# Cross-attention block: the probabilities-times-values products on 64x32 tiles of the PE array instead of 128x64 tiles with zeros in the weights

## What is computed

```
q  = layer_norm(x, ln1) @ wq + bq          # 16 heads x 32
k  = context @ wk + bk ; v = context @ wv + bv
s  = q_h . k_h / sqrt(32), masked where key > query position
p  = softmax(s)
o  = concat_h(p_h @ v_h)                   # the products that are changed
x1 = x + o @ wo + bo
y  = x1 + gelu(layer_norm(x1, ln2) @ w1 + b1) @ w2 + b2
```

## Time and profile before

| | |
|---|---|
| median of 3 runs | 1918.54 us |
| profiled execution, its own time | 1918.34 us |
| its span, first to last instruction | 1916.6 us |
| PE busy | 1820.8 us (95% of the span) |
| DVE / ACT / POOL busy | 1247.4 / 631.8 / 447.1 us |
| mean granted TensorE clock | 0.976 |

### The profile page before, as it was taken

The page is one execution under the profiler, slowest core; times in us unless marked ns, Lnnn a source line. Parts: engine busy times, 40 slices in busy tenths (PEclk is TensorE's granted clock), DMA queues, the critical chain, the costliest instruction groups (busy, mean ns, idle before and its releaser), DMA issues.

```text
span 1916.6 us, 26803 instructions
## 1 busy us (share of the span) xinstructions
PE 1820.8 (95%) x10206; PEld 852.2 (44%) x10214; DVE 1247.4 (65%) x1908; ACT 631.8 (33%) x786; POOL 447.1 (23%) x380
## 2 busy tenths in 40 slices
PE   3737999999999999999999999999999999999999
PEld 2313444444444444444444444444444444444444
DVE  5757967657576766757676665667666566766632
ACT  3434624223242422324242332424233242424211
POOL 1431314122131313213141212213141121413200
PEclk7868999999999999999999999999999999999999
DMA  7051231313323140322314042232404123230300
GB/s 280 9 124 34 44 89 23 77 35 62 72 45 88 23 88 24 69 64 44 89 26 86 23 83 51 45 88 37 96 2 88 45 50 84 45 88 8 60 23 22
DMA packets 287511, 116.48 MB, mean 61 GB/s; under 512 B 262376, under 2 KB 263952, under 8 KB 287376
## 3 DMA queue, kind: packets, MB, share of 16 engines
q1 hardware_dynamic: 287376, 114.61, 26.9%
HBM read 31.22 MB, written 16.78 MB: 25 GB/s over the span
## 4 chain that ended last, share of the span: by engine, by line
PE 89%; DVE 5%; issue 2%; DMA 2%; ACT 1%; POOL 1%; SPq 1%; DVEq 0%; POOLq 0%; ACTq 0%
PE ff_ps L1065 34%; PE ff_ps L1270 33%; PE at_ps L1065 16%; PE at_ps L1209 2%; PE at_ps L1189 2%; DMA arena<-qT 1%; DVE w_all L784 1%; DVE ssum L1006 0%; DMA arena<-in_L_xattn_wv 0%; DVE maxima L793 0%; DVE arena L784 0%; DVE xhat L773 0%; DVE stats L751 0%; DVE arena L990 0%; DVE smax L988 0%
## 5 line engine op out<-in xcount | busy, mean ns | idle before, releaser
L1065 PE MATMUL ff_ps<-arena,w_all 128*128 128x512 f16 x3072 | 701.9, 381 | 11.0 <-ACT arena L709 4.9
L1270 PE MATMUL ff_ps<-w_all,arena 128*128 128x512 f16 x3072 | 697.9, 379 | 1.7 <-DVE arena L784 1.7
L1065 PEld LDWEIGHTS ff_ps<-arena,w_all 128*128 128x128 f16 x3072 | 299.2, 98 | 378.9 <-issue 19.7
L1270 PEld LDWEIGHTS ff_ps<-w_all,arena 128*128 128x128 f16 x3072 | 294.4, 98 | 356.0 <-issue 3.0
L709 ACT ACTIVATE arena<-ff_ps,b1p,scales 128x512 f32<-128x512 f32 x256 | 198.7, 776 | 659.4 <-PE ff_ps L1065 659.1
L1038 DVE TENSOR_SCALAR arena<-arena,scales 128x512 f16<-128x512 f32 x256 | 140.9, 550 | 239.7 <-ACT arena L709 239.7
L784 DVE SCALAR_TENSOR_TENSOR arena<-arena,scales 128x512 f16<-128x512 f32 x256 | 240.1, 938 | 9.1
L477 POOL TENSOR_TENSOR rstd<-ve,minus_half 128x1 f32<-128x1 f32 x128 | 85.8, 671 | 561.7 <-DVE ve L756 554.3
L644 ACT ACTIVATE norm_hl<-xhat 128x512 f16<-128x512 f32 x120 | 73.9, 628 | 294.9 <-DVE xhat L773 294.9
L531 POOL TENSOR_TENSOR x_sb<-x_sb,bo_row 128x512 f32<-128x512 f32 x64 | 90.9, 1450 | 343.9 <-PE at_ps L1189 343.9
L536 POOL TENSOR_TENSOR arena<-arena,rsum 128x1024 f32<-128x1024 f32 x64 | 124.8, 1971 | 180.6 <-DVE rsum L1009 180.6
(11 more groups left out here) (133 smaller groups left out, 1416.3 us busy)
## 6 DMA issues: line engine op xcount, KB each, us to landing
x_sb<-in_x SPq DMA_DIRECT2D x64, 256.0 KB, 2.7
out_x<-arena SPq DMA_DIRECT2D x64, 256.0 KB, 2.3
w_all<-in_L_xattn_w SPq DMA_DIRECT2D x6, 1024.0 KB, 14.8
arena<-in_L_xattn_w SPq DMA_DIRECT2D x2, 1024.0 KB, 14.0
v_sb<-v_sb SPq DMA_DIRECT2D x6, 192.0 KB, 3.1
arena<-in_ctx SPq DMA_DIRECT2D x1, 1024.0 KB, 5.4
arena<-in_L_xattn_wk SPq DMA_DIRECT2D x1, 1024.0 KB, 8.1
arena<-in_L_xattn_wv SPq DMA_DIRECT2D x1, 1024.0 KB, 7.9
```

The costliest lines, as they stand in the source:

```text
L1065: last = nc.tensor.matmul(out_ap, s, m, start=(i == 0), stop=(i == n - 1))
L1270: last = nc.tensor.matmul(ff2_ps[:, t, :], pair[:, s, rows], m[:, j], start=(j == 0 and i == 0), stop=(j == NJ - 1 and i == 2))
```

## The change

The zeros go. Each V matmul now has the values of one head on the 64 rows on which its probabilities lie, and 32 columns; two row halves (e) by four column groups (q) make eight such tiles, and 512 columns (all four token tiles) are moved through each. Step 0 does heads 0 to 7, step 2 heads 8 to 15; steps 1 and 3 are empty on PE, but ACT and DVE still take out two banks for each. V0/V1 move from position 20 to 23 and V2/V3 from 23 to 24. The first V step now waits for all four `z_moved`, the second for the evictions of the first (`v_lo`). A PE-side increment `values_begun` stands behind the waits. POOL copies the values (`v_now`) in place of the mask product. The features of the attention output now lie in another order on the partitions, so the rows of `wo` are loaded in that order, by 16 DMAs of 32 rows instead of one of 512.

```diff
-    20: [("V", 0), ("V", 1)], 23: [("V", 2), ("V", 3)],
+    23: [("V", 0), ("V", 1)], 24: [("V", 2), ("V", 3)],
...
-            sp.dma_start(wo_raw, wo.rearrange("(k p) n -> p k n", p=P)).then_inc(w_loaded[W_O], 16)
+            for s in range(2):
+                for q in range(GH):
+                    for e in range(2):
+                        at = (8 * s + 2 * q + e) * HD
+                        sp.dma_start(wo_raw[q * HD:(q + 1) * HD, 2 * s + e], wo[at:at + HD, :]
+                                     ).then_inc(w_loaded[W_O], 16)
...
-                        nc.gpsimd.tensor_tensor(vblk[:, a], vals,
-                                                mask_v[:, :].unsqueeze(1).to_broadcast([P, NPAIR, 2 * HD]),
-                                                ALU.mult).then_inc(blk_set, 1)
+                        nc.gpsimd.tensor_copy(v_now[:, a], v_sb[:, a, bass.ds(batch, 1), :].rearrange(
+                            "p b n -> p (b n)")).then_inc(blk_set, 1)
...
-                    nc.scalar.activation(
-                        aT_hi[:, 2 * (t % 2):2 * (t % 2) + 2, (t // 2) * HALF:(t // 2 + 1) * HALF],
-                        bank.rearrange("p (m n) -> p m n", m=2), ACT.Copy, scale=1.0 / PROB_SCALE
-                    ).then_inc(v_hi, 1)
+                    nc.scalar.activation(aT_hi[:, t], bank, ACT.Copy, scale=1.0 / PROB_SCALE).then_inc(v_hi, 1)
...
-                    elif kind == "V":
+                    elif kind == "V" and t % 2 == 0:
...
-                        elif t >= 2:
-                            pe.wait_ge(v_lo, 4 * c + t - 1)
-                        if t % 2 == 0:
-                            for n in range(2):
-                                pe.wait_ge(z_moved[t + n], 16 * c + 16)
-                        for i in range(2):
-                            m = 2 * (t % 2) + i
-
-                            for n, (s, a) in enumerate(((0, 0), (0, 1), (1, 0))):
+                            for n in range(TT):
+                                pe.wait_ge(z_moved[n], 16 * c + 16)
+                        else:
+                            pe.wait_ge(v_lo, 4 * c + 2)
+                        pe.sem_inc(values_begun, 1)
+                        for n, (s, a) in enumerate(((0, 0), (0, 1), (1, 0))):
+                            for q in range(GH):
                                 for e in range(2):
+                                    half = slice(SC * e, SC * (e + 1))
+                                    head = 4 * t + 2 * q + e
                                     last = nc.tensor.matmul(
-                                        at_ps[SC * e:SC * (e + 1), t % 2, i * HALF:(i + 1) * HALF],
-                                        vblk[:, s, 2 * m + e], pT[:, t // 2 * 2:t // 2 * 2 + 2, a, KT * e + m],
+                                        at_ps[q * HD:(q + 1) * HD, e, :], v_now[half, s, head * HD:(head + 1) * HD],
+                                        pT[half, :, a, KT * (q % 2) + t + q // 2],
                                         start=(n == 0), stop=(n == 2))
-                        last.then_inc(v_ps, 1)
+                        last.then_inc(v_ps, 2)
```

More of the change, by code:

```diff
@@ L148, in cross_attention_block @@
         kblk = carve(KT * 2 * SC).bitcast(F16).rearrange("p (a g h k) -> p a g h k", a=2, g=KT, h=2)
-        vblk = carve(D).bitcast(F16).rearrange("p (a g n) -> p a g n", a=2, g=NPAIR)
+        v_now = carve(D).bitcast(F16).rearrange("p (a n) -> p a n", a=2)
         raw_at = used[0]
@@ L194, in cross_attention_block @@
         mask_k = sb("mask_k", [P, 2], F16)
-        mask_v = sb("mask_v", [P, 2 * HD], F16)
         W2_ORDER = (2, 3, 0, 1)
@@ L284, in cross_attention_block @@
         moves_begun = sem("moves_begun")
+        values_begun = sem("values_begun")
         z_moved = [sem(f"z_moved{t}") for t in range(TT)]
@@ L485, in _ @@
             reduce_maxima(1)
-            pool.wait_ge(const_dve, 2)
+            pool.wait_ge(const_dve, 1)
             for m in range(KT):
@@ L518, in key_blocks, with batch_values @@
                             ALU.mult).then_inc(blk_set, 1)
-                def value_blocks():
+                def batch_values():
                     for a in range(2):
-                        vals = v_sb[:, a, bass.ds(batch, 1), :].rearrange("p b (g n) -> p (b g) n", g=NPAIR)
-                        nc.gpsimd.tensor_tensor(vblk[:, a], vals,
-                                                mask_v[:, :].unsqueeze(1).to_broadcast([P, NPAIR, 2 * HD]),
-                                                ALU.mult).then_inc(blk_set, 1)
+                        nc.gpsimd.tensor_copy(v_now[:, a], v_sb[:, a, bass.ds(batch, 1), :].rearrange(
+                            "p b n -> p (b n)")).then_inc(blk_set, 1)
                 def add_bo():
@@ L553, in slot @@
                     pool.wait_ge(v_moved, 6 * 16)
-                    value_blocks()
+                    batch_values()
                     for n in range(2, KT):
@@ L599, in magnitudes @@
             def magnitudes(n, sums_before):
-                act.wait_ge(w_loaded[n], 16)
+                act.wait_ge(w_loaded[n], HEADS * 16 if n == W_O else 16)
                 wait(act, sums_ready, sums_before)
@@ L735, in _ @@
             nc.vector.memset(mask_k[:, :], 0.0).then_inc(chain, 1)
-            nc.vector.memset(mask_v[:, :], 0.0).then_inc(chain, 1)
             nc.vector.memset(minus_half[:, :], -0.5).then_inc(chain, 1)
-            links[0] += 3
-            dve.wait_ge(chain, 3)
+            links[0] += 2
+            dve.wait_ge(chain, 2)
             for h in range(GH):
                 last = nc.vector.memset(mask_k[HD * h:HD * (h + 1), h % 2:h % 2 + 1], 1.0)
-            last.then_inc(const_dve, 1)
-            for r in range(2):
-                last = nc.vector.memset(mask_v[SC * r:SC * (r + 1), HD * r:HD * (r + 1)], 1.0)
             last.then_inc(const_dve, 1)
@@ L1014, in step @@
                         dve.wait_ge(v_hi, 4 * c + t + 1)
-                        cut = (slice(None), slice(2 * (t % 2), 2 * (t % 2) + 2),
-                               slice((t // 2) * HALF, (t // 2 + 1) * HALF))
-                        low(aT_lo[cut], bank.rearrange("p (m n) -> p m n", m=2), 1.0 / PROB_SCALE, aT_hi[cut], v_lo)
+                        low(aT_lo[:, t], bank, 1.0 / PROB_SCALE, aT_hi[:, t], v_lo)
                     elif kind == "O":
@@ L1149, in _ @@
             pe.wait_ge(const_set, 2)
-            pe.wait_ge(const_dve, 3)
+            pe.wait_ge(const_dve, 2)
             def slot(c, par, attn, ff, batch):
```

## The result

The changed kernel takes 1901.28 us (median of 4 runs, 1899.53 to 1902.16), the kernel before 1918.13 us on the same chip (4 runs, 1916.04 to 1918.78). The ratio is 0.9914, 95% interval 0.9902 to 0.9926: faster by 14 to 19 us. The forecast was 1905.5 us, with a range from 1900.5 to 1912.0; the direction and the range held, and the middle was 4.2 us too high.

The account below looks back on a forecast made before the run. PE, busy 95% of the span and 89% of the chain of waits, was taken as the bound. -17.6 + 3.0 - 0.9 + 0.3 + 2.4 = -12.8 us from 1918.34 gives 1905.5 us; range 1900.5 to 1912.0.

Parts of the forecast that it names:

- 1, slots 2 to 15: Slots 2 to 15: 28 V blocks shrink from 1.43 to 0.80 us, -17.6 us, if no new wait appears.
- 2, slot 0: Slot 0: both V blocks and the evictions between them come after the last landing, unhidden, at half clock; +3.0 us.
- 3, POOL's copy: POOL in slot 0: two copies of the values cost 1.36 us instead of 2.26 for the products; -0.9 us.
- 4, slot 1 at full clock: Slot 1: the first V block, free before, now comes after the transposes' landing; +0.3 us.
- 4, the clock: Slot 1: PE idles about 5.4 us and its granted clock falls to 0.50; +2.4 us.
- 5, loads: Start: 16 DMAs of `wo` delay `w1` and `w2` by up to 10 us, but nothing is late; cost 0.
- (a): Check on z_moved[3], slots 2 to 15: last transpose lands before PE reaches position 23; slack 0.4 us, 0.14 of it transit.
- (b): Check on `v_lo` between the V blocks: evictions done after 2.93 us, PE back after 3.50, so covered.
- (c): Check on `v_lo` ahead of O: 2.93 us of block and evictions against 0.80 + 2.70, so covered.
- A: Rival: the clock does not fall in slot 1, 1903.1 us; its chance is within the forecast's shared 0.70.
- B: Rival: a new short wait in each slot, +7.0 us at 0.5 us in 14 slots, 1912.5 us; chance 0.16.
- C: Rival: row halves take turns or weight loads bind, V block stays 1.43 us; +8.6 us, 1926.9 us; chance 0.10.

Follow-up runs that it names:

- the early block: The changed kernel with V0/V1 at position 22 instead of 23; 1919.71 us in a single run.
- the eight matmuls of filling: The changed kernel with other banks in slot 0, slot 1's V blocks at 24 and 25, and 8 thrown-away matmuls ahead of slot 1's wait; 1907.67 us.
- the copy undone: The changed kernel with POOL multiplying the values by a tile of ones in place of the copy; 1903.14 us.
- with filling: The changed kernel with 20 thrown-away matmuls of 512 columns on PE in slot 1, ahead of the wait for the transposes; 1899.35 us.
- the split load alone: The kernel before with only `wo` loaded by 16 DMAs of 32 rows, in natural order; 1914.95 us, ratio 0.9994.
- the plan alone: The kernel before, old tiles and zeros kept, with V0/V1 moved to position 23 and V2/V3 to 24; 1912.73 us, ratio 0.9976.

## Why the prediction was right, and where it was not

**Bound and block.** The chain showed V blocks back to back with other PE work, so shortening them had to shorten the end, and it did. The block came out at 0.77 us, forecast 0.80; three rounds of 0.216 leave 0.12 for filling and draining, as in the S block. Eight tiles cost next to nothing beyond two. By the Trainium skill's page TensorE: Matmul & The Clock Gate, section Measured speedup vs the span model, each further tile would add about 4 ns; for the six tiles beyond a pair that is an estimated 0.02 us, so 0.80 and not the prediction's 0.81. The trace agrees with the spacing: the first eight matmuls of a block start within 0.03 us (the window of L1206 below), 3 to 4 ns from each other; the block as a whole took 0.77.

```profile
348.22:348.26 0.04, 0.03 (x8) 0.03 (x9) 1.00 0.00 0
```

The Trainium skill's page TensorEngine Tiling (Array Packing), section Gotcha 2, holds that column tiling does without the fast weight load; the trace can't say how a weight was loaded, but at 0.77 us a block no load is the limit.

**The terms**, each against what the runs show:

| term | forecast | measured | from |
|---|---|---|---|
| 1, slots 2 to 15 | -17.6 | -17.5 | mean of 7 traces with the new tiles and the same loop (1534.7 to 1537.7) less mean of 4 with the old (1552.1 to 1554.2); left out are the row halves in turn (1536.5), the early block (1552.5) and the eight matmuls of filling (1546.7) |
| 2, slot 0 | +3.0 | +3.05 on PE; to POOL's deviations +3.6 in the pair, +3.1 between means | landing to O 4.41 and 7.46; landing to `rstd` 17.25 and 20.82 (17.0 to 17.6, mean 17.3, with the old tiles; 19.9 to 20.8, mean 20.4, with the new and the same banks) |
| 3, POOL's copy | -0.9 | -0.3 to -0.6 | the copy undone |
| 4, slot 1 at full clock | +0.3 | +0.4 | 6.76 and 7.18 (with filling) |
| 4, the clock | +2.4 | +2.4 when it falls | 9.55 and 7.18 |
| 5, loads | 0 | within -3.3 and +0.8 | the split load alone |
| not in the sum | | -0.8 | first issue to last landing in slot 0: 19.1 to 19.3 with the new tiles; 19.85, 20.20 and 19.85 with the old plan; 19.39 with the plan alone |

The profiled pair alone gives 19.2 for term 1. The tiles account for 28 x 0.66 = 18.5 of it. The rest is PE's one wait for DVE in slot 2, 1.70 us before and 0.81 after; the pauses at the loop's turns took 0.2 us more than before.

**The checks.** (a) held: in slots 2 to 15 PE waited for no transpose. The first block started 0.60 to 1.12 us behind the landing, 0.24 of which is the way to PE: a slack of 0.36 to 0.88 us, where 0.4 less 0.14 was forecast for slot 2 (0.38 there). The experiment that took it away showed how near this was. (b), (c): first V block at 348.23, DVE's second eviction of it done at 349.78 + 1.29 = 351.07, so 2.84 us (forecast 2.93), and PE back at 351.70. These are the rows:

```profile
349.78 1.29 DVE L781 SCALAR_TENSOR_TENSOR act_T<-at_ps,act_T 128x512 f16<-128x512 f32 x2 [1.94 <-ACT act_T L670]
```

**The step that failed** is in term 4, though its size was right: "The granted clock was still 1.00 through the 3.42." One execution was taken for the kernel's behaviour. Of three traces with the old plan and 3.4 us of idle time (3.42, 3.40, 3.39) the clock fell in one. Of five with 5.6 us and no filling it fell in all five. So the change seems to raise the chance of a drop that the kernel already had, and the cost belongs to it only in part; eight traces are few. A second term was mis-sized: POOL's copy, -0.9 in the forecast, gave 0.3 to 0.6. The two copies take 1.69 us where 1.36 was taken from the nearest row, so that they are only 0.57 shorter than the products. The Trainium skill's page TensorE: Matmul & The Clock Gate, Part 1, says that idleness returns the clock to half; the traces agree as far as direction goes.

**The 4 us by which the middle was high.** For the profiled pair the table of stretches adds up without a rest:

| stretch, us | forecast | profiled pair | second execution of before against after |
|---|---|---|---|
| start to landing in slot 0 | -0.9 | -4.3 | +0.7 |
| landing to O in slot 0 | +3.0 | +3.05 | +3.05 |
| O of slot 0 to O of slot 1 | +2.7 | +3.5 | +0.7 |
| O of slot 1 to O of slot 15 | -17.6 | -19.2 | -19.4 |
| O of slot 15 to the end | 0 | 0 | 0 |
| sum | -12.8 | -16.9 | -15.0 |

So 3.4 us of the miss lie in the start and 1.6 in the loop, and 0.8 came back in slot 1. The start is spread and not the change: slot 0's last landing lies between 119.6 and 124.8 us over all traces of kernels with the original or the 16-part load, and the trace first shown of the kernel before is the latest of them; the next is at 122.5. The clock's fall in slot 1 of the kernel before has no part in this pair, since it held there; in the second execution it fell, and slot 1 costs the change only 0.7 us more.

Worked from the terms instead, the sum is -17.5 + 3.1 - 0.8 - 0.5 + 0.4 + 2.4 = -12.9 us against an execution of the kernel before whose clock holds, and -15.6 (2.7 less) against one whose clock falls too. The interval of the measurement ends at -14.2. The medians of the unchanged kernel in later sets of runs, 1916.1 to 1917.6 us, are 0.5 to 2 us under the 1918.13 that the result is measured against. So the terms were right to about a microsecond each, and that the middle missed by only 4 us says little about them: a different draw of the start moves it by as much.

**The rivals.** A (the clock holds in slot 1) did not come, though filling brings it about. B did not come; one position earlier it does. C, turns in place of overlap, is refuted by the 0.77 and again by the 0.80 with the halves in turn. What stays open: `values_begun` was never taken out alone, so that its cost is nothing is only consistent with the 0.11 us between a V block and its neighbour staying (2.69 against the earlier trace rows's 2.70).

## What to carry to other kernels

Zeros in stationary weights are array time: if the operands already lie on separate row groups, smaller tiles side by side can halve a product's time, and where the chain shows it back to back with other work, the gain comes through one for one, provided that whatever now comes later (here the last transpose, with 0.4 to 0.9 us to spare) stays ahead of it. A fill or drain slot in which nothing hides the waits has to be costed by itself: here slot 0 gave back a sixth of what slots 2 to 15 gained, and slot 1 nearly as much again in the executions in which the clock falls only with the change. And one trace is one draw: a second profile of the unchanged kernel would have changed two terms of this reading, so take it before explaining a few microseconds.

## What the runs showed that I had not expected

- Two row halves of the array overlap even when the program issues all twelve matmuls of one half ahead of the other's (0.80 against 0.77 us).
- The clock fell after idle times of 2.96 and 3.39 us, and once after a pause of 2.08 with one of 0.42 shortly ahead, and held after 3.07, 3.40 and 3.42: length alone doesn't decide it.
- With eight more matmuls ahead of a loop, 11 us more were spent inside it: pauses of 1.7 to 2.1 us at each turn, 8.7 us more in all, and one fall of the clock. Why is not shown.
- POOL's pause behind a cross-partition maximum was 6.7 to 7.8 us at 75 to 84 us, when the weight loads had landed, and 11.53 at one place with loads in flight (7.05 at another); a copy issued behind the maximum ran ahead of the pause, a product behind it.
- Four loads that gather distant rows, 4 x 256 KB, delayed the later weight loads by 8 us (last landing 50.07 against 42.14); with sixteen of 32 adjoining rows each it was 41.5 to 42.6 us, with one load 39.6 to 40.5.
